# A five-pass graph kernel on one core: first loads of the masked layer, its turnover from the second hop, and the last rows

## What is computed

```python
# layer 0:  Ax = adj @ h;  x = x + 1 - 0.1*h - 0.01*sum(h*Ax, axis=1)
# layer 1, two hops:
for k in range(2):
    h = tanh(concatenate([adj @ h, h], 1) @ W[k])
# x = x + h
# layer 2, masked:
mask = (adj != 0)
rank = cumsum(mask, axis=1); deg = rank[:, -1:]
k = minimum(deg, 100); pos = rank - (deg - k)
w = mask * where(pos > 0, 0.5 ** (k - pos), 0)
# x = x + w @ (h @ weight) + bias
# layer 3: u_intra = tanh([h, t] @ W1 + b1) @ W2 + b2
#          x = x + u_intra + adj @ (h @ B.T) - rowsum(adj) * (h @ B.T)
```

## Time and profile before

| | |
|---|---|
| median of 3 runs | 698.91 us (698.21 to 699.77) |
| profiled execution, its own time | 700.7 us |
| span of its trace, first to last instruction | 698.9 us |
| TensorE clock granted | 1.0 of full speed throughout |
| busy: PE, DVE, ACT, POOL | 668.3, 469.6, 192.5, 114.2 us |
| DMA | 256.51 MB, mean 367 GB/s |

### The profile page before, as it was taken

The page is one execution under the profiler, slowest core; times in us unless marked ns, Lnnn a source line. Parts: engine busy times, 40 slices in busy tenths (PEclk is TensorE's granted clock), DMA queues, the critical chain, the costliest instruction groups (busy, mean ns, idle before and its releaser), DMA issues.

```text
span 698.9 us, 10418 instructions
## 1 busy us (share of the span) xinstructions
PE 668.3 (96%) x3811; PEld 270.2 (39%) x3824; DVE 469.6 (67%) x813; ACT 192.5 (28%) x296; POOL 114.2 (16%) x132
## 2 busy tenths in 40 slices
PE   3999999999999999999999998899999999999997
PEld 1434433334433333333344443444444443333332
DVE  7777767777899999996888888899989810000000
ACT  1101111011111001101111116899998811111111
POOL 4110011110200000001222223222332211211111
PEclk9999999999999999999999999999999999999999
DMA  8999999998589999959999983999999479999992
GB/s 347 422 410 411 413 412 409 418 414 335 190 329 388 420 422 419 415 206 402 384 406 420 419 368 134 362 378 408 414 414 412 191 263 341 417 415 418 417 419 98
DMA packets 42098, 256.51 MB, mean 367 GB/s; under 512 B 5120, under 2 KB 11264, under 8 KB 11840
## 3 DMA queue, kind: packets, MB, share of 16 engines
q1 hardware_dynamic: 38712, 252.85, 89.6%
q10 hardware_dynamic: 3336, 3.00, 1.5%
HBM read 252.28 MB, written 3.54 MB: 366 GB/s over the span
## 4 chain that ended last, share of the span: by engine, by line
PE 53%; DMA 20%; DVE 19%; POOL 4%; issue 3%; ACT 0%; SPq 0%; DVEq 0%; ACTq 0%; POOLq 0%
PE accA L1373 37%; DMA cache<-adj_blocks 10%; DVE uS L1111 8%; DMA land<-adj_blocks 6%; PE accA L1424 4%; PE work L1408 4%; DVE uS L1155 3%; POOL rstd L762 2%; DMA rows_transposed<-rowsT 2%; PE work L1391 1%; PE work L1336 1%; POOL tS L772 1%; PE accA L1342 1%; PE work L1267 1%; PE work L1304 1%
## 5 line engine op out<-in xcount | busy, mean ns | idle before, releaser
L1373 PE MATMUL accA<-land,X 128*64 128x512 f32 x1568 | 374.1, 598 | 13.6 <-DVE X L1197 11.3
L1373 PEld LDWEIGHTS accA<-land,X 128*64 128x64 f32 x1568 | 110.6, 137 | 193.7 <-issue 166.9
L1155 DVE TENSOR_SCALAR uS<-land 128x1024 bf16<-128x1024 f32 (+1 forms) x196 | 134.5, 730 | 30.1 <-DMA land<-adj_blocks 28.4
L1111 DVE TENSOR_TENSOR uS<-uS,land 128x512 f32<-128x512 f32 x178 | 125.2, 704 | 9.6
L1373 PE MATMUL accA<-cache,X 128*64 128x512 f32 x480 | 120.1, 598 | 2.6 <-DMA cache<-adj_blocks 2.6
L591 ACT ACTIVATE wS<-work 128x1024 uint16<-128x1024 f32 x114 | 109.2, 1037 | 8.8 <-PE work L1408 8.7
L769 POOL TENSOR_TENSOR hS<-tS 128x256 f32<-128x256 f32 x24 | 23.5, 978 | 400.5 <-DVE tS L979 400.5
L1097 DVE TENSOR_TENSOR zS<-uS,work 128x256 f32<-128x256 f32 x8 | 3.4, 421 | 123.1 <-PE work L1267 106.9
L1408 PE MATMUL work<-uS,triA 128*128 128x512 bf16 x248 | 74.4, 380 | 2.2 <-DVE uS L1155 1.8
L1424 PE MATMUL accA<-wS,X 128*128 128x512 bf16 x251 | 74.7, 379 | 0.3
L850 ACT ACTIVATE accS<-accA 128x512 f32<-128x512 f32 x32 | 19.1, 598 | 177.3 <-PE accA L1373 165.5
(11 more groups left out here) (109 smaller groups left out, 417.4 us busy)
## 6 DMA issues: line engine op xcount, KB each, us to landing
land<-adj_blocks SPq DMA_DIRECT2D x221, 1024.0 KB, 10.3
cache<-adj_blocks SPq DMA_DIRECT2D x15, 1024.0 KB, 16.7
xin<-x_rows ACTq DMA_DIRECT2D x8, 128.0 KB, 7.6
out_rows<-zS ACTq DMA_DIRECT2D x8, 128.0 KB, 6.9
uS<-counts ACTq DMA_DIRECT2D x60, 4.0 KB
x_rows<-zS SPq DMA_DIRECT2D x7, 128.0 KB, 11.4
rows_transposed<-rowsT SPq DMA_DIRECT2D x7, 128.0 KB, 8.6
wS<-rows_transposed SPq DMA_DIRECT2D x7, 128.0 KB, 8.5
```

The lines of the kernel that those rows point to most:

```text
L1111: nc.vector.tensor_tensor(total, total, of[:, i * W:(i + 1) * W], ALU.add)\
L1155: nc.vector.tensor_scalar(masks(p, c, b)[0:rows, :], block_of(p, c, b)[0:rows, :], 0.0, None, ALU.not_equal)\
L1373: last = nc.tensor.matmul(accA[k * D:(k + 1) * D, c % 2, :], tile(X[p % 2], TQ * q + k), of[:, k * W:(k + 1) * W], start=(b == 0), stop=(b ...
```

## The change

SyncE no longer has the counts transfer that needs the fold (`counts_for(3)`) ahead of the first load of L2's second chunk, nor the left-over rows of the last chunk in its queue; ScalarE issues those, and it also issues the transposed rows. The totals of L1B's last chunk, their fold and the masks 0, 1 and 2 of L2 now lie in that chunk's own steps. Stages of L1A, L1B and L2's first chunk come a block earlier, the left-over weights of L0's last chunk two or three. VectorE makes the weights of block 8 and 13 in L2's first chunk too. The join of L2 is done in one stage with eight 64-wide pieces. The last chunk's sums, result and store go in two halves. The diff, without blank lines, most unchanged lines and the helpers `last_nat`, `last_half` (two banks and two halves for the last sums) and `last_stages` (which now names the new stages):

```diff
--- before.py
+++ after.py
@@ -230,12 +230,21 @@
 def evac_on_dve(c):
-    return (3, 13) if c else ()
+    return (3, 13) if c else (8, 13)
 EVAC_STEP = {13: 12}
+MASKS_AHEAD = {10: 0, 12: 1, 14: 2}
+LAST_TOTALS = {14: 12}
+LAST_FOLD = 13
@@ -283,15 +292,15 @@
              "left": 16, "turn": 17, "turned": 17, "left out": 18, "hop": 19, "hopped": 20}
-STAGES_L1A = {1: 2, "added": 4, "tanh": 6, "hop": 8, "hopped": 10}
-STAGES_L2 = {0: 2, "join0": 4, "join1": 5, 4: 5, 5: 7, 6: 10, 7: 13, 8: 15}
-STAGES_L1B = {1: 3, "added": 5, "tanh": 6, 3: 7, 4: 8, 5: 10, "turn": 12, "turned": 13, 6: 14, 8: 15}
+STAGES_L1A = {1: 2, "added": 3, "tanh": 5, "hop": 8, "hopped": 10}
+STAGES_L2 = {0: 2, "join": 4, 4: 5, 5: 7, 6: 10, 7: 13, 8: 15}
+STAGES_L1B = {1: 2, "added": 4, "tanh": 5, 3: 6, 4: 7, 5: 11, "turn": 12, "turned": 13, 6: 14, 8: 15}
 QUICK = {L1A: {0: 0, 1: 1, 3: 1, 4: 1, 5: 1, 6: 2, 7: 5, "turn": 10, "turned": 10, "hop": 11, "hopped": 12, "part": 13,
          L1B: {1: 1, "added": 2, "tanh": 3, "hop": 5, "hopped": 6},
-         L2: {"tanh": 0, 4: 0, 5: 2, "turn": 8, "turned": 9, 6: 10, 7: 10, 8: 11,
-              "row sums": 14},
+         L2: {"tanh": 0, "join": 1, 5: 1, "turn": 7, "turned": 7, 6: 9, 8: 9, "left rows": 13,
+              "row sums": 12},
          L3: {0: 0, 1: 1, 4: 3, 5: 5, 6: 6, 7: 8, 8: 10}}
@@ -306,7 +315,7 @@
 ROWS_KEPT = {6: 5, 8: 4, 9: 6, 10: 3, 12: 2, 14: 1}
-LEFT_L1A = {"counts": 2, "weights": 3, "left": 5, "left out": 7}
+LEFT_L1A = {"counts": 0, "weights": 1, "left": 2, "left out": 4}
 SUM_STAGES = {"sums": 3, "result": 7, "store": 11}
...
@@ -608,6 +625,13 @@
             eng.dma_start(xin[:, :], chunk(x3_d, c)).then_inc(rows_in, 16)
+        def left_rows_of(eng, c):
+            eng.wait_ge(copy_used, copied_no(L1B, c, 1) + 1)
+            eng.dma_start(loS[4 * c:4 * c + 4, :], chunk(X[1], c)[LAST:P, :].bitcast(F16)).then_inc(left_rows, 16)
         def rows_store(eng, p, c):
@@ -645,16 +669,6 @@
                 sp.dma_start(left_weights(c), left_d[ch(L2, c)]).then_inc(left_in[c % 2], 16)
-            def left_rows_of(c):
-                sp.wait_ge(copy_used, copied_no(L1B, c, 1) + 1)
-                sp.dma_start(loS[4 * c:4 * c + 4, :], chunk(X[1], c)[LAST:P, :].bitcast(F16)).then_inc(left_rows, 16)
-            def keep_rows(c):
-                sp.wait_ge(tr_evac, tr_no(L2, c) + 1)
-                sp.dma_start(hT_d[ch(L2, c)], rowsT[:, :]).then_inc(hT_out, 16)
             def rows_back(c):
@@ -666,18 +680,13 @@
             def after_masks(g):
-                if issued["keep"] < NC - 2 and g >= PAIRS * (issued["keep"] + 2) + 2:
-                    keep_rows(issued["keep"])
-                    issued["keep"] += 1
                 if issued["left"] < NC and g >= PAIRS * (issued["left"] - 1) + 3:
                     issued["left"] += 1
-                if issued["left rows"] < NC and g >= LEFT_ROWS_AT[issued["left rows"]]:
-                    left_rows_of(issued["left rows"])
-                    issued["left rows"] += 1
-            LEFT_ROWS_AT = {NC - 3: 1, NC - 2: 3, NC - 1: 7}
-            issued = {"keep": 0, "left": 2, "left rows": NC - 3}
+                if g == 1:
+                    left_rows_of(sp, NC - 2)
+            issued = {"left": 2}
             def step(p, c, before, before2):
@@ -691,11 +700,10 @@
                     left_over(1)
-                    counts_for(3)
+                    left_rows_of(sp, NC - 3)
                 if p == L3 and c == 0:
                     after_masks(PAIRS * NC - 1)
-                    keep_rows(NC - 2)
                 if p == L0:
@@ -707,8 +715,10 @@
                     load(p, c, k)
+                    if (p, c, j) == (L2, 1, 0):
+                        counts_for(3)
                     if p == L1B and c >= 3 and j == 1:
-                        left_rows_of(c - 3)
+                        left_rows_of(sp, c - 3)
                     if p == L3 and c >= 3 and j == 0:
@@ -876,6 +886,9 @@
                     rows_transposed(p, c)
+                    if p == L2 and c < NC - 1:
+                        act.wait_ge(tr_evac, tr_no(p, c) + 1)
+                        act.dma_start(hT_d[ch(p, c)], rowsT[:, :]).then_inc(hT_out, 16)
                 if at == 8 and p in (L1B, L2):
@@ -893,6 +906,19 @@
                                          bias=hbias[:, h:h + 1]).then_inc(hidden_ready, 1)
+                if at == "last sums":
+                    act.wait_ge(intra_done, c + 1)
+                    act.wait_ge(swept, sweep_no(p, c) + 1)
+                    act.wait_ge(nat_done, nat_no(p, c))
+                    for h in range(2):
+                        nc.scalar.activation(accS[:, h * CH:(h + 1) * CH], accA[:, c % 2, h * CH:(h + 1) * CH], ACT.Copy)\
+                            .then_inc(acc_evac, 1)
+                if at == "last store":
+                    for h in range(2):
+                        act.wait_ge(nat_evac, nat_no(p, c) + 1 + h)
+                        act.dma_start(last_half(chunk(out, ch(p, c)), h), last_half(zS, h)).then_inc(rows_out, 16)
+                if at == "left rows":
+                    left_rows_of(act, c)
                 if at == ("store" if p == L3 else 7) and p in rows_to and not rows_by_sync(p, c):
...
@@ -1089,6 +1115,13 @@
                     side = sideS[:, (c % 2) * CH:(c % 2 + 1) * CH]
+                    if at == "last result":
+                        dve.wait_ge(side_ready, c + 1)
+                        rows_written()
+                        for h in range(2):
+                            dve.wait_ge(nat_done, nat_no(p, c) + 1 + h)
+                            nc.vector.tensor_tensor(last_half(zS, h), last_half(side, h), last_nat(h), ALU.add)\
+                                .then_inc(nat_evac, 1)
                     if at == "result":
@@ -1097,20 +1130,16 @@
             def main(p, c, b):
-                if b in totals_at(p, c):
-                    wait_landed(dve, p, c, b, first=True)
-                    of, total = block_of(p, c, b), totals(ch(p, c))
-                    if b == totals_at(p, c)[0]:
-                        if p == L1A and c == 0:
-                            dve.wait_ge(counted, NQ * NC)
-                        nc.vector.tensor_tensor(total, of[:, 0:W], of[:, W:BLK], ALU.add).then_inc(totalled, 1)
-                    else:
-                        for i in range(TQ):
-                            dve.wait_ge(totalled, totalled_no(p, c, b) - TQ + i)
-                            nc.vector.tensor_tensor(total, total, of[:, i * W:(i + 1) * W], ALU.add)\
-                                .then_inc(totalled, 1)
-                    if b == totals_at(p, c)[-1] and (p, c) != (L1B, NC - 1):
+                if (p, c) == (L1B, NC - 1):
+                    for k in totals_at(p, c):
+                        if LAST_TOTALS.get(k, k) == b:
+                            add_totals(p, c, k)
+                    if b == LAST_FOLD:
+                        fold_totals(p, c)
+                        nc.vector.tensor_tensor(part_sums, part_sums, more_sums, ALU.add).then_inc(folded, 1)
+                elif b in totals_at(p, c):
+                    add_totals(p, c, b)
+                    if b == totals_at(p, c)[-1]:
                         fold_totals(p, c)
@@ -1118,10 +1147,26 @@
                             weights_out(dve, nc.vector, c, k)
+                if (p, c) == (L1B, NC - 1) and b in MASKS_AHEAD:
+                    mask(L2, 0, MASKS_AHEAD[b])
                 if p == L2 and NQ * c + b + LEAD < NQ * NC:
                     weights_out(dve, nc.vector, c, b)
+            def add_totals(p, c, b):
+                wait_landed(dve, p, c, b, first=True)
+                of, total = block_of(p, c, b), totals(ch(p, c))
+                if b == totals_at(p, c)[0]:
+                    if p == L1A and c == 0:
+                        dve.wait_ge(counted, NQ * NC)
+                    nc.vector.tensor_tensor(total, of[:, 0:W], of[:, W:BLK], ALU.add).then_inc(totalled, 1)
+                else:
+                    for i in range(TQ):
+                        dve.wait_ge(totalled, totalled_no(p, c, b) - TQ + i)
+                        nc.vector.tensor_tensor(total, total, of[:, i * W:(i + 1) * W], ALU.add)\
+                            .then_inc(totalled, 1)
             def fold_totals(p, c):
@@ -1157,18 +1202,12 @@
                 if p == L2 and c == 0:
-                    for b in range(2):
-                        mask(p, c, b)
-                    fold_totals(L1B, NC - 1)
-                    nc.vector.tensor_tensor(part_sums, part_sums, more_sums, ALU.add).then_inc(folded, 1)
                     epilogue("added", before)
-                    for b in range(2, 4):
-                        mask(p, c, b)
+                    mask(p, c, 3)
                     epilogue(3, before)
-                    for b in range(4, LEAD):
-                        mask(p, c, b)
-                for k, e in early_stages(p, c, before, before2):
-                    epilogue(k, e)
```

(28 more changed lines are left out.)

10 lines of the change are left out of this document (6 added, 4 removed).

## The result

The changed kernel takes 694.58 us (median of four runs, 694.41 to 695.13), the kernel before 699.34 us beside it on the same chip (698.21 to 700.38): 4.8 us less. The ratio is 0.9924, with a 95% interval of 0.9907 to 0.9941; it is estimated from all runs and is not the quotient of the two medians (0.9932). The interval leaves 1 out, so the kernel is faster, and the time is inside the range, but 3.1 us above the 691.5 us forecast. The profiled execution has a span of 693.3 us against 698.9.

What follows compares the result with a forecast made beforehand. Memory was taken to bound the masked pass, VectorE's round the second hop. Gains of 5.0 + 1.2 + 0.4 + 0.5 + 0.35 = 7.45 us took 700.7 to 693.3; less 1.8 for the median, 691.5 us, range 687.0 to 696.5.

Steps and rivals of the forecast that it cites:

- Hop 2: Second hop (L1B): VectorE's round falls below TensorE's 15.07 us; 3.2 us gained, bounds 0 and 3.9.
- The counter-rule: Second hop: VectorE and GpSimd block each other fully, so moved totals wait and the hop gains next to nothing.
- Rival two: Second hop not shortened, by blocking engines or late loads: 3.2 us lost, 694.7 us, chance 0.18.
- The turnover: Start of L2: first eight loads 5.0 us earlier on average, hop's 3.2 included; full memory is ahead by that.
- Memory faster: Masked pass, 450 to 490 us: more loads under way raise the rate from 390 towards 414 GB/s; 1.2 us gained.
- the last masked chunk: End of masked pass: engines behind the last loads gain 0.4 us from join and turn.
- rival one: Masked pass: memory isn't the bound, the engines decide; 687.7 us, chance 0.2.
- L3's join and the halves: L3's first chunk gains 0.5 us from the new join; the last sums in halves gain 0.35 us.
- L1A: Second join: a 1.6 us wait replaces one of 0.88; the 0.8 us loss is hidden by a load wait.
- ScalarE: Masked pass: waiting for and issuing transposed rows takes 0.8 us a chunk, within 1.7 us free.
- Left-over rows and block 8: First masked chunk: TensorE's 1.6 us wait for rows goes, VectorE's weights come 1.3 us late; one pays the other.
- Rivals three and four: Three: first loads not early, 698 us, chance 0.08. Four: ScalarE bounds the masked pass, 702 us, chance 0.06.

Runs made afterwards that it cites:

- e7: Kernel before with only the second hop's stage table of the changed kernel: 694.93 us, ratio 0.9929.
- e2: Changed kernel with masks 0 and 1, the last totals and the fold again behind the last sweep: 694.62 us, ratio 0.9927.
- g1: Changed kernel with counts in pieces of 1 KB and masks 0 and 1 both at block 12: 691.43 us, ratio 0.9876.
- e1_hop_undone: Changed kernel with the second hop's stage table as before: 698.64 us, ratio 0.9991.
- e8_no_evac: Changed kernel with all weights of the first masked chunk made by ScalarE, as before: 694.84 us, ratio 0.9928.
- e5: Changed kernel loading 1 KB instead of 4 KB of counts from the masked pass's fifth block pair on, output partly wrong: 690.90 us, ratio 0.9870.
- e3: Changed kernel with the left-over stages and first hop's stages in L1A as before: 694.41 us, ratio 0.9929.
- e4: Changed kernel with the masked pass's transposed rows stored from SyncE's queue again: 694.79 us, ratio 0.9927.
- f2: Changed kernel with each 4 KB load of counts split into four packets of 1 KB: 693.16 us, ratio 0.9902.

## Why the prediction was right in sign and 3.1 us off

**Hop 2: right.** Forecast 3.2 us, bounds 0 and 3.9. The table alone gives 3.9 us (e7), the changed kernel keeps 2.7 us, since mask 0 waits for the last landing ahead of `hS` (1.2 us where 0.5 was taken, and 0.5 to 1.4 us in the other kernels that keep it; e2 and g1 without that wait have the full 3.9). The counter-rule was weighed rightly in its effect: the totals do not wait for the inverse root, which takes 1.39 us while three totals beside it take 0.69 us each, as alone. The scaling takes 1.05 us beside totals, and in the last chunk, where VectorE waits, this:

```profile
415.33 0.61 POOL L782 TENSOR_TENSOR tS<-tS,rstd 128x256 f32<-128x256 f32 x1
```

It loses 0.44 us, and the total that meets it 0.29. The Trainium skill (SBUF — State Buffer, "Who interferes with whom") says that this pair contends for shared ports and that the lock on them is exclusive; it does not say for how much of an instruction it is held. The prediction's rule took it as held for the whole of each. The scaling does not contradict even that: it starts at 370.10 us, when the third total has 0.58 us left, and the fourth total starts when the scaling has 0.44 us left, so neither loses more than the rest of the other. The inverse root does contradict it, as no total beside it loses anything. Rival two falls.

**The turnover, 1.8 us: this step failed.** Its mechanism was that a full memory is ahead by the average lead of the first eight loads, put at 5.0 us, 1.8 beside the hop. The first load came nearly as forecast (6.8 us earlier with the scatter taken off, 7.5 forecast). The others did not. Beside the hop, the first eight loads are 0.8 us earlier on average and not 1.8, and the seventh, which was to gain 3 us or more once the left-over rows left the queue, gained nothing: it goes out 19.2 us behind the copy before and 19.4 after, now waiting for a mask, as VectorE makes weights ahead of its masks.

```profile
442.00 0.33 SPq L763 DMA_DIRECT2D land<-adj_blocks  x1
```

Six kernels with the same burden on the memory, times against the copy that ends hop 2, in us:

| kernel | first load | third load | mean of the first eight | masked pass |
|---|---|---|---|---|
| before | 2.28 behind | 6.76 behind | 11.0 behind | 135.47 |
| e7_before_hop | 0.33 behind | 6.41 behind | 10.4 behind | 135.32 |
| e1_hop_undone | 0.33 ahead | 6.87 behind | 10.9 behind | 135.52 |
| e2_turnover_undone | 1.68 ahead | 6.93 behind | 10.8 behind | 135.69 |
| after | 1.84 ahead | 6.35 behind | 10.3 behind | 135.05 |
| e8_no_evac | 1.85 ahead | 6.34 behind | 9.3 behind | 135.44 |

The first load moves over 4.1 us, and the pass over 0.6 and not in that order: the lead of the first load is worth nothing. In the first five the mean moves over 0.8 us only, too little to tell whether the pass follows it. In e8 it is 1.7 us less than before, nearly the forecast, and the pass is as long as before. So the second half of the step fails too in the one kernel that had the lead (its second chunk takes 17.86 us where the changed kernel's takes 15.81, and why it does was not found). SyncE's loads wait for VectorE's masks: a load needs a place that masks free, and the third and later ones depend on the last chunk's rows, which come a set time behind the copy. The row of landings 434 to 446 us after says the same: the memory is not full there but has nothing to do,

```profile
land<-adj_blocks SPq DMA_DIRECT2D x5, 1024.0 KB, 5.3
```

5.3 us where the earlier trace rows had 7.6. The lead of the first two loads is spent in these gaps (share 0.89 from 430 to 450 us where before it was 0.96). That the waiting part of the sum is set by places and not by the start was in the code, and I had not followed it past the second load.

**Memory faster, 1.2 us, and the last masked chunk, 0.4: the rate rose as taken, the time did not come.** From 450 to 490 us it moves 410 GB/s, where half of the way from 390 to 414 was assumed. Chunks there take 15.6 to 15.8 us in place of 16.0. But then come 16.41, 17.04 and 17.17 us, before 16.78 and 17.49: landings reach 15 us with the 25th load of the pass instead of the 34th, and the full memory takes it back. The last chunk takes 14.86 us where it took 13.64, 1.2 us more and not 0.4 less: its data come late. The step held the bound to be bytes a second. It is the late engine, whose chain of packets ends 6 us behind most others (under e5): 15.7 us of landing at 415 GB/s, and with smaller counts the chunks stay at 15.62 us and 4.7 us go (e5). So rival one was nearer in kind than it looked: with most of the burden gone no engine waits for a load and the engines decide, but that is another kernel than this change.

**L3's join and the halves: right**, 0.71 us (0.5 forecast) and 0.28 (0.35). The join after:

```profile
559.30 0.64 PE L1291 MATMUL accA<-wts,accS 128*64 128x64 f32 x16
...
689.88 0.69 PE L1300 MATMUL work<-wts,accS 128*64 128x64 f32 x16 [0.62 <-ACT accS L914]
```

These 1.0 us pay for the 1.2 us that mask 0 costs in hop 2, which is why e7 and the changed kernel are equal. By the profile the change is worth 2.70 + 0.42 + 0.71 + 0.28 = 4.1 us; the interval of the ratio runs from 4.1 to 6.5 us. That these two are real is read from the profile alone; they were not run apart. Of the 3.1 us by which the forecast is off, 2.7 are gain that did not come (4.8 of 7.45 us in the medians); 0.4 is the base, for the kernel before took 699.34 us beside the changed one and the forecast started from 698.91.

**L1A: right**, a wait of 1.60 us at the second join against the 0.88 us of the earlier trace rows, hidden as argued (e3). **ScalarE**: no bound; e4 shows that even 8.2 us of waits in the pass cost nothing. **Left-over rows and block 8**: TensorE does not wait for the rows any more, and 0.96 us for block 8's weights (1.3 forecast); e8 shows no difference. Rivals three and four fall with the first load at 420.75 us and with the chunks at 15.6. Two of the rivals' sums were slightly off, which changes nothing above: rival one's first masked chunk is 1.6 + 2 - 1.3 = 2.3 us and not 2.1, and rival three's terms give 696.9 to 697.9 us and not 698.

**What stays open.** Why four or 16 small packets win only a third of what one small packet wins. In the changed kernel a second engine is late too (to 547.35 us) without a counts packet in its chain, and in f2 one is late to 547.65; what holds it up was not found. The completion writes, which grow with the pieces, would be one reason, the other small transfers of those engines another; neither was tried apart. And how much of g1's gain over f2 is mask 0 and how much the chip, as the two ran on different ones.

## What to carry to other kernels

A transfer that starts early helps only as far as there are free places behind it: follow the third and the fourth, not the first. Before a full memory is taken for bytes a second, look at the stretch behind the last load: if a small share stays busy while loads are still out, one engine is late, and transfers of a single packet are the first suspects. And run the one table line alone before adding ten edits to it: here it gave as much as all of them.

## What the runs showed of the hardware

Eight transfers of 4 KB a chunk, each one packet, lengthen the masked pass from 130.3 us, with a quarter of their size, to 135.1, while they are under 0.5% of its bytes (32 KB of the 7 MB that a chunk of 17 us moves at 415 GB/s). The engine whose chain of packets has them in it finishes last in the changed kernel, at 550.17 us, while most of the 16 are done by 544. Spread over four or 16 packets they cost about two thirds of it still. A landing time at full memory is that of the slowest engine, and was 15.7 or 12.7 us at the same 415 to 418 GB/s. Three VectorE additions beside GpSimd's power on 128x4 (1.39 us) took 0.69 us each, as alone; one beside GpSimd's scaling of 128x256 took 0.98, and the scaling 1.05 in place of 0.61.
